# Two maxima of the first layer moved into the projections' bank in tiles 5 and 6, and 26 unread products taken out

## The chip, the cores and the metric

The kernel runs on one core of a Trainium2 chip. The metric is the device time of one execution in microseconds. TensorE is called PE, VectorE DVE, ScalarE ACT, GpSimd POOL and the engine that issues the loads SP, as in the profile.

## What is computed

A perceiver of two layers works on 128 query rows of width 256 against a context of 12544 rows. Each layer begins with a cross attention of 16 heads of width 16; in the first a mask is added to the scores. Between the attentions lie a causal linear attention, a GELU block and a ternary feed-forward block; behind the second lie an RWKV mixing and a ternary convolution block.

```python
q = split_heads(ln(x) @ Wq.T + bq)               # 128 rows
k = split_heads(ctx @ Wk.T + bk)                 # 12544 rows
v = split_heads(ctx @ Wv.T + bv)
scores = einsum('bhqd,bhkd->bhqk', q / 4, k)     # first layer: + (1 - mask) * -10000
out = einsum('bhqk,bhkd->bhqd', softmax(scores), v)
x = x + L0_xattn; x = x + L0_attn; x = x + L0_ffn
x = x + L1_xattn; x = x + L1_attn; x = x + L1_ffn
```

## The kernel before

The context is cut into NB = 14 blocks of 896 rows, each into 7 tiles of 128. Blocks are numbered m = 0 to 27: 0 to 13 in the first layer, 14 to 27 in the second. The softmax runs online: before the scores of a block are computed, its maximum over the 896 rows is needed for every head and query. It comes from 32 **maxima** a block (16 heads, two halves of 448 rows): `maximum` on PE (L1081) multiplies the high halves of queries and keys into a bank of PSUM, and DVE reduces that to one column (L753, with the mask added, in the first layer; L756 in the second). Here `J` counts them, and `max_free` says that DVE has read one.

The maxima of block m+1, and the first of block m+2, are spread over the tiles of block m. A tile is, in PE's order: `scores` (the row maxima subtracted, L1118, then the scores, L1122), the maxima "behind the scores", `weigh` (the values weighed with the probabilities of the tile before, L1139), the maxima "behind the weighing", `projections` (keys L1064 in tiles 0, 2, 4, 6, values L1054 in tiles 1, 3, 5, in the bank `ps_proj`; in tile 5 a piece of the values before that into a lent bank of `ps_scores`, and in tile 6 four products that turn the new maxima, L1156, into the same lent bank), and the maxima "ahead", always two. In tile 1 the sums of the block before are turned in `ps_proj` (L1150), and DVE adds them (L802). `count_at` gives the numbers by tile from `SCORED_AT` and `WEIGHED_AT`. All engines follow one table, `MAXIMA`; `MAX_BANK` says which bank a product goes to: 0 and 1 are the two halves of `ps_max`, used in turn, 2 is `ps_proj`, which then has to be free of its last reader (`proj_free`).

The other engines in a tile of the first layer: DVE adds the mask to the scores of eight heads (L811), ACT copies the other eight (L539) and POOL adds the mask to them (L426); ACT takes the exponentials (L546), copies keys (L507), values (L514) and sums (L530) out of PSUM. At tile 5 DVE makes the chain of the block's maximum: L769, L772, L779. POOL besides prepares the mask (L395), the ternary weights (L407, L409, L411), the high halves of the keys (L417) and decays the sums (L437). A load into a mask or context buffer is issued by SP in the order of the blocks, and waits for the last use of that buffer.

Block 13 has no maxima and no projections; its scores alternate between banks, and DVE adds all of the mask (L822). Between the layers, projections for blocks 15, 16, 14 and 15 fill PE's waits (`between_in`). The first maxima of the second layer are read in pairs of halves (`pair_maximum`, L764).

`idle_products(n, bank)` (L1211) issues n products of 128x256 fp32 that nobody reads; each is two records in the trace.

Of the kernel before, what the change touches and what calls it, by code (L numbers as in the profile page):

```python
# [17 lines left out]
TILES = 7  # L18
KB = TILES * P
NB = SK // KB  # L20
# [15 lines left out]
def perceiver(nc, a, out):  # L36

    with ExitStack() as ctx:
# [13 lines left out]
        ps_proj = ctx.enter_context(nc.psum_tensor("ps_proj", [P, 512], F32))  # L52
# [127 lines left out]

        SCORED_AT = ((2, 0, 2, 1, 2, 0, 0), (2, 1, 2, 2, 2, 2, 2))
        WEIGHED_AT = ((1, 2, 1, 2, 1, 2, 2), (0, 2, 1, 1, 0, 1, 0))
        LAST_AT, SUMS_AT = 5, 1
# [17 lines left out]
        for l in range(2):  # L201
            done, read = {NB * l: 2 * H}, {bank: 2 * H * (NB * l + 1) for bank in range(2)}
            turn_of = 0
            for m in range(NB * l, NB * (l + 1)):
                for t in range(TILES):
                    now, ahead = count_at(m, t)
                    MAXIMA[m, t] = []
                    for k in range(3):
                        here = []
                        for to, count in ((m + 1, now[k]), (m + 2, ahead[k])):  # L210
                            at = done.get(to, 0)
                            here += [(to, j) for j in range(at, at + count)]
                            done[to] = at + count
                        for i, (to, j) in enumerate(here):
                            if m > 0 and k == 0 and len(here) == 2 and i == 0 and (t != SUMS_AT or m == NB):
                                MAX_BANK[to, j] = 2
                            else:
                                MAX_BANK[to, j], MAX_AFTER[to, j] = turn_of, read[turn_of]
                                read[turn_of] = 2 * H * to + j + 1
                                turn_of = 1 - turn_of  # L220
                        MAXIMA[m, t].append(here)
# [469 lines left out]
        def _(dve):  # L691
# [140 lines left out]
            for l in range(2):  # L832
# [26 lines left out]
                for n in range(NB):  # L859
                    m = NB * l + n  # L860
                    for t in range(TILES):
                        behind_scores, behind_weighing, ahead = MAXIMA[m, t]
                        early = behind_scores if l == 1 or m == 0 else behind_scores[0:1]
                        for k, j in early:
                            maximum(k, j)
                        if l == 0 and is_last(m):
                            bias_last(m, t)
                        elif l == 0:
                            bias_first(m, t)
                        for k, j in behind_scores[len(early):]:  # L870
                            maximum(k, j)
# [157 lines left out]
        def _(pe):  # L1029
# [97 lines left out]
            def weigh(m, t):  # L1127
# [7 lines left out]
                for half in (first, 1 - first):  # L1135
                    pe.wait_ge(sig(f"exp_done{half}"), T + 1)
                    for j, h in enumerate(HEADS[half]):
# [3 lines left out]
                                  skip_group_check=True)  # L1141
                    if m == NB - 1 and half == first and SUMS_AT <= t < TILES - 1:
                        proj_free(None)
                        idle_products(1, ps_proj)
                last.then_inc(sig("pv_done"), 1)
# [73 lines left out]
            for l in range(2):  # L1219
# [32 lines left out]
                else:  # L1252
                    for i in range(H):
                        pair_maximum(NB, i)
                        if i in BESIDE_AT:
                            beside_in(BESIDE_AT.index(i))
                        elif i > 5:
                            idle_products(1, ps_out)
                        if i == 5:
                            for u in range(len(BESIDE)):  # L1260
                                beside_read(u)
                read_by[0] = ("max_copied", NB * l + 1)
                idle_products(2 + 2 * l, ps_proj)
                turn_max(NB * l)
# [4 lines left out]
                for n in range(NB):  # L1269
                    m = NB * l + n  # L1270
                    for t in range(TILES):
# [18 lines left out]
                        for k, j in ahead:  # L1290
                            maximum(k, j)
                if l == 0:
                    idle_products(2, ps_proj)
                weigh(NB * l + NB - 1, TILES - 1)
# [6 lines left out]
                if l == 0:  # L1301
# [48 lines left out]
                    between_in(10, 11, 12)  # L1350
                    idle_products(1, ps_proj)
                    pe.wait_ge(sig("hq_made"), 1)
                    for c in range(FC):
                        last = tr(ps_max[:, 0, :].bitcast(BF16)[:, P * c:P * (c + 1)], xq[:, P * c:P * (c + 1)], ident16[:, :])
                    last.then_inc(sig("hq_turned"), 1)
                    idle_products(2, ps_proj)
                    pe.wait_ge(sig("hq_ready"), 1)
# [115 lines left out]
```

## Time and profile before

| what | value |
|---|---|
| three runs | 1075.67, 1073.76, 1072.72 us (median 1073.76) |
| profiled execution | 1068.03 us, its span 1066.3 us |
| mean granted clock of PE | 0.992 |
| busy, share of the span | PE 95%, DVE 70%, ACT 64%, POOL 39% |
| DMA | 53.31 MB, mean 50 GB/s |
| a block of the first layer | 33.73 us |

The profile is of one execution. The granted clock is 1 where PE runs at its full 2.4 GHz and 0.5 where it runs at 1.2. A PE that is called busy is not PE at its peak: the ends of products are modelled, and neighbours overlap.

### The profile page before, as it was taken

How to read it: one execution, taken by the hardware profiler on the slowest of the kernel's cores; microseconds unless marked ns; L12 is line 12 of the kernel's file. 1: busy time of each engine (PE TensorE's matmuls, PEld its weight loads, DVE VectorE, ACT ScalarE, POOL GpSimd, SP SyncE). 2: the span in 40 equal slices, each digit the busy share in tenths (PEclk: the TensorE clock that was granted, in tenths of full speed). 3: DMA queues.
4: the chain of work that ended last, by engine and by line, in shares of the span. 5: the costliest groups of instructions: out<-in, count | busy, mean ns of one | idle time of the engine just before them, and what ended most of it. 6: DMA issues, size and time to landing. Idle time of an engine off the chain costs nothing. (4 is left out here: it accounts for less than half of the span.)

```text
span 1066.3 us, 30777 instructions
## 1 busy us (share of the span) xinstructions
PE 1017.6 (95%) x12921; PEld 687.8 (65%) x12921; DVE 743.1 (70%) x1715; ACT 679.0 (64%) x953; POOL 420.8 (39%) x374
## 2 busy tenths in 40 slices
PE   8899999999999999998878899999999999999876
PEld 5466666676666666665544566667676666666665
DVE  4888888888888888876357666556665565566465
ACT  3677777777778777876542555566556666555722
POOL 4368888888888988881000000101100101000000
PEclk9999999999999999999998999999999999999999
DMA  8420122201221112112031010111100111000000
GB/s 313 140 71 20 54 70 71 67 23 53 71 72 34 45 65 70 53 66 93 10 120 68 2 36 2 37 36 37 36 8 30 37 37 36 2 2 2 2 1 5
DMA packets 14682, 53.31 MB, mean 50 GB/s; under 512 B 3025, under 2 KB 4817, under 8 KB 13649
## 3 DMA queue, kind: packets, MB, share of 16 engines
q1 hardware_dynamic: 14544, 51.35, 14.0%
q8 instruction: 102, 1.67, 0.7%
q14 instruction: 36, 0.29, 0.1%
HBM read 51.21 MB, written 0.13 MB: 48 GB/s over the span
## 5 line engine op out<-in xcount | busy, mean ns | idle before, releaser
L756 DVE TENSOR_REDUCE tile_max<-ps_max 128x1 f32<-128x448 f32 x339 | 200.7, 620 | 150.7 <-PE ps_max L1081 146.5
L753 DVE CUSTOM_DVE_ANT_0 unread<-ps_max,masks 128x448 bf16<-128x448 f32 x396 | 231.4, 621 | 67.4 <-PE ps_max L1081 66.2
L426 POOL TENSOR_TENSOR probs<-probs,masks 128x512 f32<-128x512 f32 x182 | 228.1, 1275 | 72.0 <-ACT probs L539 70.5
L551 ACT ACTIVATE probs<-ps_scores 128x1024 f32<-128x1024 f32 x193 | 187.2, 1021 | 86.2 <-PE ps_scores L1122 86.1
L546 ACT ACTIVATE probs<-probs 128x1024 f32<-128x1024 f32 x196 | 207.4, 1058 | 54.5 <-DVE probs L811 45.7
L1122 PE MATMUL ps_scores<-q_pad,k_full 32*128 32x256 f32 x3088 | 230.6, 377 | 0.0
L1139 PE MATMUL ps_out<-probs,values 128*32 128x128 f32 x6272 | 214.5, 277 | 0.7 <-ACT probs L551 0.4
L1139 PEld LDWEIGHTS ps_out<-probs,values 128*32 128x32 f32 x6272 | 159.4, 110 | 51.7 <-issue 48.0
L1122 PEld LDWEIGHTS ps_scores<-q_pad,k_full 32*128 32x128 f32 x3088 | 191.4, 186 | 0.7
L1081 PE MATMUL ps_max<-k_high,q_high 32*128 32x448 bf16 x735 | 180.1, 358 | 7.9 <-DVE tile_max L756 5.3
L1064 PE MATMUL ps_proj<-ctx_t,wk 128*128 128x448 f32 x384 | 168.8, 562 | 0.0
L417 POOL CAST k_high<-k_full 128x896 bf16<-128x896 f32 x56 | 52.3, 935 | 262.1 <-ACT k_full L507 262.1
L1054 PE MATMUL ps_proj<-wv,ctx_t 128*128 128x256 f32 x608 | 148.9, 388 | 0.0
L1081 PEld LDWEIGHTS ps_max<-k_high,q_high 32*128 32x128 bf16 x735 | 48.4, 91 | 140.8 <-issue 70.2
L1054 PEld LDWEIGHTS ps_proj<-wv,ctx_t 128*128 128x128 f32 x608 | 111.3, 190 | 23.4 <-issue 8.0
L811 DVE TENSOR_TENSOR probs<-ps_scores,masks 128x1024 f32<-128x1024 f32 x91 | 111.1, 1221 | 1.6 <-PE ps_scores L1122 1.4
L1118 PE MATMUL ps_scores<-max_rows,minus 32*128 32x512 bf16 x772 | 103.8, 382 | 4.8 <-ACT max_rows L525 3.4
L514 ACT COPY values<-ps_proj 128x512 f32<-128x512 f32 x76 | 44.5, 586 | 98.5 <-PE ps_proj L1054 98.3
L539 ACT COPY probs<-ps_scores 128x512 f32<-128x512 f32 x182 | 97.3, 589 | 1.5 <-PE ps_scores L1122 1.4
L1064 PEld LDWEIGHTS ps_proj<-ctx_t,wk 128*128 128x128 f32 x384 | 65.1, 189 | 50.1 <-issue 43.7
L432 POOL TENSOR_TENSOR max_step<-max_wide 128x16 f32<-128x16 bf16 x28 | 6.9, 246 | 225.5 <-DVE max_wide L779 225.5
L507 ACT ACTIVATE k_full<-ps_proj,bk 128x448 f32<-128x448 f32 x96 | 60.9, 635 | 40.3 <-PE ps_proj L1064 38.2
(258 smaller groups left out, 914.4 us busy)
## 6 DMA issues: line engine op xcount, KB each, us to landing
ctx_t<-in_ctx_t SPq DMA_DIRECT2D x28, 896.0 KB, 5.3
masks<-in_mask_n SPq DMA_DIRECT2D x14, 448.0 KB, 3.4
masks<-in_mask_t SPq DMA_DIRECT2D x14, 448.0 KB, 3.5
room_w<-in_L_attn_f_w SPq DMA_DIRECT2D x2, 1024.0 KB, 7.5
room_w<-in_L_ffn_w SPq DMA_DIRECT2D x2, 1024.0 KB, 8.8
room_w<-in_L_ffn_w_gate SPq DMA_DIRECT2D x1, 1024.0 KB, 10.6
room_w<-in_L_ffn_w_up SPq DMA_DIRECT2D x1, 1024.0 KB, 13.1
room_w<-in_L_ffn_w_down SPq DMA_DIRECT2D x1, 1024.0 KB, 15.0
```

The costliest lines, as they stand in the source:

```text
L426: nc.gpsimd.tensor_tensor(p, p, three(mask_t[m % 2], TILES)[:, t, :].unsqueeze(1).to_broadcast([P, 4, P]), ALU.add).then_inc(sig("bias_add ...
L546: nc.scalar.activation(prob(T, half), prob(T, half), ACT.Exp).then_inc(sig(f"exp_done{half}"), 1)
L551: nc.scalar.activation(prob(T, half), scores_half(T, half), ACT.Exp).then_inc(sig(f"exp_done{half}"), 1)
L753: ins = v.tensor_tensor_reduce(unread[:, j % 2, :], max_bank(m, j)[:, 0:HALF], mask_n[m % 2][:, HALF * half:HALF * (half + 1)], 1.0, -3e38 ...
L756: ins = v.tensor_reduce(tile_max[:, h, half:half + 1], max_bank(m, j)[:, 0:HALF], AX_X, ALU.max)
L811: v.tensor_tensor(prob(T, 0).rearrange("p (h q) -> p h q", h=8), ps_scores[:, 0:2, :].rearrange("p a (h q) -> p (a h) q", q=P), three(mask ...
L1054: last = mm(bank[:, D * (t - at.start):D * (t - at.start + 1)], ctx_t[m % 3][:, c, P * t:P * (t + 1)], wv[l][:, c, :], start=(c == 0), sto ...
L1064: last = mm(bank[:, 0:HALF], wk[l][:, c, P * oc:P * (oc + 1)], ctx_t[m % 3][:, c, HALF * half:HALF * (half + 1)], start=(c == 0), stop=(c ...
L1081: mm(max_bank(m, j)[:, 0:HALF], q_high[rows, c, zz, :], k_high[m % 2][rows, c, HALF * half:HALF * (half + 1)], start=True, stop=True).then ...
L1118: mm(banks[g], minus16[rows, :], max_rows[m % 2][rows, :], start=True, stop=True)
L1122: last = mm(banks[g][:, D * c:D * (c + 1)], k_full[m % 3][rows, c, P * t:P * (t + 1)], q_pad[rows, c, :], start=False, stop=True, skip_gro ...
L1139: last = mm(ps_out[VW * g:VW * (g + 1), P * c:P * (c + 1)], values[m % 2][:, t, h, :], prob(T, half)[:, P * o:P * (o + 1)], start=(t == 0 ...
```

## The change

Per block of the first layer, the maxima behind the weighing fall from 1 to 0 in tiles 0 and 2, and those behind the scores rise from 0 to 1 in tiles 5 and 6; their total stays 32. The function `late_bank` sends the ones of tiles 5 and 6 into `ps_proj`, and `before_mask` has DVE read them behind its mask addition. The functions `idle_products` in block 13 (5 products), among the pairs (10), before the turning of the first maxima (2 and 4), before the last weighing of the first layer (2) and around the gated products (3) are taken out. Those of the tail remain, as do the small products (`idents`) at the start.

```diff
-        SCORED_AT = ((2, 0, 2, 1, 2, 0, 0), (2, 1, 2, 2, 2, 2, 2))
-        WEIGHED_AT = ((1, 2, 1, 2, 1, 2, 2), (0, 2, 1, 1, 0, 1, 0))
+        SCORED_AT = ((2, 0, 2, 1, 2, 1, 1), (2, 1, 2, 2, 2, 2, 2))
+        WEIGHED_AT = ((0, 2, 0, 2, 1, 2, 2), (0, 2, 1, 1, 0, 1, 0))
+        def late_bank(m, t):
+            return m < NB and t >= LAST_AT
+
+        def before_mask(m, t, count):
+            return 0 if late_bank(m, t) else count if m == 0 or m >= NB else min(count, 1)
...
-                            if m > 0 and k == 0 and len(here) == 2 and i == 0 and (t != SUMS_AT or m == NB):
+                            if k == 0 and (late_bank(m, t) or m > 0 and len(here) == 2 and i == 0 and (t != SUMS_AT or m == NB)):
                                 MAX_BANK[to, j] = 2
...
-                        early = behind_scores if l == 1 or m == 0 else behind_scores[0:1]
-                        for k, j in early:
+                        early = before_mask(m, t, len(behind_scores))
+                        for k, j in behind_scores[:early]:
                             maximum(k, j)
...
-                        for k, j in behind_scores[len(early):]:
+                        for k, j in behind_scores[early:]:
                             maximum(k, j)
...
-                    if m == NB - 1 and half == first and SUMS_AT <= t < TILES - 1:
-                        proj_free(None)
-                        idle_products(1, ps_proj)
...
-                        elif i > 5:
-                            idle_products(1, ps_out)
...
-                idle_products(2 + 2 * l, ps_proj)
...
-                if l == 0:
-                    idle_products(2, ps_proj)
...
-                    idle_products(1, ps_proj)
                     pe.wait_ge(sig("hq_made"), 1)
...
-                    idle_products(2, ps_proj)
                     pe.wait_ge(sig("hq_ready"), 1)
```

## Rows read from the trace of the kernel before

**Rows 1.** Busy time by stretch: block 7 of the first layer, its tile 6; columns: stretch, length, busy.

```profile
310.12:343.86 33.74, 33.51 (x453) 22.57 (x454) 28.36 (x75) 26.43 (x39) 27.93 (x24) 1.00 0.17 57
...
339.01:343.86 4.85, 4.63 (x69) 2.81 (x70) 3.40 (x9) 4.05 (x6) 3.50 (x5) 1.00 0.21 80
```

**Rows 2.** Timeline, tiles 0 to 3 of block 7: start, duration, engine, line, tiles.

```profile
312.51 0.36 PE L1081 MATMUL ps_max<-k_high,q_high 32*128 32x448 bf16 x1
...
312.79 1.77 PE L1064 MATMUL ps_proj<-ctx_t,wk 128*128 128x448 f32 x4
...
314.50 0.46 PE L1081 MATMUL ps_max<-k_high,q_high 32*128 32x448 bf16 x2
...
314.70 0.47 PE L1118 MATMUL ps_scores<-max_rows,minus 32*128 32x512 bf16 x4
...
314.93 0.64 ACT L507 ACTIVATE k_full<-ps_proj,bk 128x448 f32<-128x448 f32 x1
...
315.97 0.66 PE L1150 MATMUL ps_proj<-ident,out_t 128*128 128x128 f32 x4
...
319.79 0.36 PE L1081 MATMUL ps_max<-k_high,q_high 32*128 32x448 bf16 x2
...
319.80 0.57 PE L1118 MATMUL ps_scores<-max_rows,minus 32*128 32x512 bf16 x4
...
324.24 0.38 PE L1081 MATMUL ps_max<-k_high,q_high 32*128 32x448 bf16 x2
...
324.36 0.48 PE L1118 MATMUL ps_scores<-max_rows,minus 32*128 32x512 bf16 x4
```

**Rows 3.** Timeline, tiles 5 and 6 of block 7.

```profile
335.76 2.50 POOL L426 TENSOR_TENSOR probs<-probs,masks 128x512 f32<-128x512 f32 x2
...
336.23 0.62 DVE L753 CUSTOM_DVE_ANT_0 unread<-ps_max,masks 128x448 bf16<-128x448 f32 x1
...
336.77 0.62 DVE L753 CUSTOM_DVE_ANT_0 unread<-ps_max,masks 128x448 bf16<-128x448 f32 x1
...
337.66 0.64 DVE L772 TENSOR_SCALAR block_max<-block_max 128x16 f32<-128x16 f32 x1
338.23 1.50 POOL L411 TENSOR_SCALAR tern<-room_w 128x512 bf16<-128x512 f32 x1
...
341.81 0.62 DVE L753 CUSTOM_DVE_ANT_0 unread<-ps_max,masks 128x448 bf16<-128x448 f32 x1
...
341.95 0.40 PE L1156 MATMUL ps_scores<-ident,max_wide 128*128 128x128 bf16 x4 [0.22 <-DVE probs L811]
...
342.19 1.72 PE L1064 MATMUL ps_proj<-ctx_t,wk 128*128 128x448 f32 x4
```

**Rows 4.** Timeline, a tile of block 13.

```profile
491.56 2.19 ACT L546 ACTIVATE probs<-probs 128x1024 f32<-128x1024 f32 x2 [0.78 <-DVE probs L822]
...
493.27 2.35 DVE L822 TENSOR_TENSOR probs<-ps_scores,masks 128x1024 f32<-128x1024 f32 x2 [0.61 <-PE ps_scores L1122]
...
493.57 0.70 PE L1211 MATMUL ps_proj<-wq,ident 128*128 128x256 f32 x2
...
494.20 0.65 PE L1139 MATMUL ps_out<-probs,values 128*32 128x128 f32 x16
```

**Rows 5.** Timeline, DVE in the pairs before the second layer's first block.

```profile
563.21 2.08 DVE L764 TENSOR_REDUCE tile_max<-ps_scores 128x2 f32<-128x896 f32 x2
...
569.42 2.20 DVE L764 TENSOR_REDUCE tile_max<-ps_scores 128x2 f32<-128x896 f32 x2
```

**Rows 6.** Busy time by stretch, with PE's clock; the last two are of PE alone.

```profile
34.90:38.30 3.40, 2.10 (x19) 1.37 (x22) 1.82 (x9) 3.01 (x6) 1.12 (x2) 1.00 0.54 153
...
574.90:579.03 4.13, 2.11 (x29) 1.14 (x27) 1.56 (x3) 2.63 (x4) 0.91 (x2) 1.00 0.00 0
...
579.86:586.25 6.39, 5.67 (x59) 0.50 0.01 3
...
591.76:595.86 4.10, 3.51 (x60) 1.00 0.02 4
```

## The prediction

> **What bounds it now.** I read first the busy times by stage, then each engine's timeline through one block of the first layer, then the stretches around the removed products. In a block PE is busy 33.51 of 33.74 us, DVE 28.36, ACT 26.43, POOL 27.93 [rows 1]. So PE's order of work sets the pace of blocks 1 to 12, and a product taken out of PE's stream is worth its slot, as long as DVE, ACT and POOL, four fifths full, don't hold the next product. Only tile 6 has a hole in PE: there it is busy 4.63 of 4.85 us [rows 1]. Around the layers PE waits for others; there the removed products lie, and they cost slots in two places only.
>
> **Part 1: tiles 0 and 2 lose their middle maximum.** In tile 0 the lone product behind the weighing starts at 312.51, the keys' projection at 312.79: a slot of 0.29 us (the two starts unrounded) [rows 2]; tile 2 has the same pair. A second effect: of the pair behind the projection the second product waits for the bank that the middle maximum held. In tile 0 the scores start 0.20 us behind that pair, in tile 2 0.12, where after tile 1 it is 0.01 [rows 2]. Without the middle maximum both banks are free, so tile 0 may gain up to 0.29 + 0.19 = 0.48, tile 2 0.29 + 0.11 = 0.40. What is late next in tile 0 is ACT: its keys copy runs 314.93 to 315.57, behind other work of ACT, and releases the turning of the sums, now at 315.97 [rows 2]; the bank allows at most 315.62, so 0.35 of the 0.48 arrives. Tile 2 has no such turn: I take 0.39. Together -0.74 a block; bounds 0 (ACT and DVE pass nothing on) and -0.88.
>
> **Part 2: one maximum more in tiles 5 and 6, in ps_proj.** Behind the scores PE takes one in at nearly no slot: it sits on 32 rows that the scores leave one after another. Bounds 0 and the 0.29 of a slot; I take 0.05, nearer to the scores' own packing, and in tile 6 it is hidden by PE's hole. But DVE reads it only behind the mask addition, and the next projection writes the same bank.
> In tile 5 the values' projection into the lent score bank comes first, so ps_proj is free in time. DVE's two later reads and the chain move back: the mask addition ends the DVE stretch and the reads stand 0.54 to 0.55 apart (336.23, 336.77) [rows 3]; with the new one in front, which DVE can start some 0.17 before the present first, the second old read moves by 0.38 to 337.15, and L772, now 337.66, is issued at about 338.04. There it matters that L772 runs 0.64 us: it ends at 338.30, just behind POOL's pair of additions (335.76 + 2.50 = 338.26) [rows 3]. It is blocked until then already, so arriving at 338.04 it ends at the same 338.30 and the 0.38 costs nothing. The margin is 0.22.
> In tile 6 nothing hides it. DVE's next read behind the mask addition starts at 341.81, PE's turning products, which wait for that addition, at 341.95, the keys at 342.19 [rows 3]. The new read takes the place at 341.81, ends about 0.55 + 0.08 later, and only at 342.50 can the keys write ps_proj: +0.31 us, on the path, since PE has nothing else queued. Everything behind it (the pair ahead, its reads, the scores of the next tile 0) moves with it. The bounds are 0 and the whole read plus a handover, 0.65.
> The sum by blocks: blocks 1 to 11, 11 x (-0.74 + 0.31 + 0.01) = -4.6; block 12, which has no maximum ahead in tile 6, -0.7; block 0, only tile 6, +0.3. Together -5.0 us. The 0.05 of tile 5 mostly falls into the wait of the borrowed bank, hence 0.01. No DMA and no wait of SP is moved: the mask's next load waits for the same count of maxima, an SP step with a block of slack.
>
> **A rule that speaks against it.** L772 is seen held up to POOL's end in the trace [rows 3]. The Trainium skill, SBUF — State Buffer, section "Who interferes with whom", says that the engine that issues first gets the port pair that DVE and POOL share for its whole instruction. The trace agrees for L772. By that rule a link that came after 338.26 would sit behind POOL's next instruction; this is rival B.
>
> **Part 3: 26 unread products.** Each is two records; one takes a slot of 0.63 us in block 13 (493.57 to 494.20) [rows 4]. There ACT's two exponentials end at 493.75 and the second half of the weighing starts at 494.20 [rows 4]; without the product it can start at 493.80. That half and the scores two tiles on come 0.40 earlier, 0.20 a tile, for five tiles: -1.0. DVE isn't reached: its two additions take 2.35 us and it is idle 0.61 before them [rows 4]. Before layer 2's first block two of DVE's double reads take 2.08 us at the start of the row of pairs and 2.20 late in it [rows 5], so spacing 1.00 against 1.11: PE paces the last six: -0.6. Four more products end at about 574.84 and hold the turning by 0.15. Together -1.7; bounds 0 and -2.2. The others lie in waits: 2 behind the first maxima, 2 before the last weighing (ACT is late there), 3 around the gated products. Each is free, and cover is lost for one thing only, the clock.
>
> **Part 4: the clock.** After 574.90 to 579.03, in which PE was busy 2.11 of 4.13 us, the granted clock fell to its lower level, 1.2 of 2.4 GHz. The tile from 579.86 then took 6.39 us at 0.50, where a full-clock one took 4.10 [rows 6]: 0.36 us lost for each us of low clock inside tiles. The stretch 34.90 to 38.30 shows 2.10 of 3.40 busy at clock 1.00 [rows 6]; without its two products some 1.1 remain, emptier than the stretch before which the clock fell. Likewise before the last weighing (two products fewer, PE then waits for ACT twice), around the gated products (three fewer), and through the sixteen pairs (ten plus four fewer). I expect more low stretches in each, but not always. Price of one: at 34.90 3 to 10 us low, 1.2 to 3.7 lost, over half of the runs, some of which have it already: +1.0. At 502, the turning and four projections in front of the normed vector: +1.2 (0 to 2). At 546: +0.4 (0 to 1.5). At the pairs DVE paces, so only the first tile's scores and the turning are late, and the low stretch that follows now may only come sooner: +0.4 (-1 to 1.8). Sum +3.0, bounds 0 and 9.
> TensorE: Matmul & The Clock Gate in the Trainium skill, section "What's actually happening", says that activity releases the throttle, the low level being the default. By this alone all four places would fall every time, and the sum would be at its upper end.
>
> **The sum.** -5.0 - 1.7 + 3.0 = -3.7 us. The profiled execution took 1068.03 (span 1066.3 and 1.7 around it); it gives 1064.3. The median of the three runs is 1073.76, 5.7 us above the profiled one, probably with a low stretch more; the terms apply to them as well: 1073.76 - 3.7 = 1070.0.
>
> **Rivals.**
> A. The clock eats the gain (0.25). For it: four emptied places [rows 6]. Against: the long blocks are dense and untouched. With 6 to 9 us lost, 1073 to 1076, no change or slightly slower.
> B. The chain misses its place behind POOL (0.08; this is the one that ends slower). Place: L772 in tile 5 of blocks 1 to 12. If DVE arrives more than 0.22 us later than I count, POOL's next instruction, 1.50 us from 338.23 [rows 3], runs first; L772 then ends at 339.9 instead of 338.30, 1.6 later. DVE's wait for the pair ahead takes up some of that; I take four fifths, 1.3, for the mask addition of tile 6, the turning and the keys. 12 x 1.3 = +15.6: about 1086. It decides from 0.22 us on; below, nothing.
> C. ACT and DVE pass on nothing of tiles 0 and 2 (0.10): the 0.31 x 12 = +3.7 stands alone, 3.7 - 1.7 + 3.0 = +5.0, 1078.8. Against: PE's 99% in the block [rows 1].
> D. The clock costs nothing (0.17): -6.7, 1067.1.
> The forecast itself, the gain in the blocks and a middling clock, has 0.40, with a range of its own of 1068 to 1072.
>
> **Range and chances.** About 0.3% (3.2 us) is what a measurement of this kernel can tell from no change. From D's 1067 with a little more from the bounds of part 1 (1065.5), up to A and C (1079); B is left out with the tails. Faster: D and four fifths of the forecast, 0.50. Same: the rest of it and most of A, 0.30. Slower: B, C and a little of A, 0.20.
>
> **What would show it.** Tile 0 and tile 2 about 0.35 to 0.4 shorter, tile 6 0.3 longer, tile 5 equal; the block 33.3 instead of 33.74. L772 still ending with POOL's additions. Block 13 near 2.8 us a tile. DVE's pairs spaced 1.00. Low stretches at one or more of 36, 503, 546 and from 565 on. It would be wrong if tile 0's gain stopped at ACT's copy, if the keys of tile 6 waited longer than 0.3, or if low stretches lay inside the blocks.

## The result and the profile after

The changed kernel takes 1068.43 us (median of 20 runs, 1064.00 to 1072.92), the kernel before 1072.39 (20 runs, 1067.88 to 1075.67). The ratio is 0.996, with an interval of 0.9944 to 0.9976: 4.0 us or 0.4% faster. The forecast was 1070.0 from 1073.76, a gain of 3.7.

The two profiled executions say nothing of the kind: 1067.97 us after, 1068.03 before, the span 1066.3 in both. Their granted clocks differ, 0.978 against 0.992. Before's profile is one of its quickest runs, after's is an ordinary one. So I compare the two by stretches first, and take the clock up separately.

A tile's length is taken from the first score product (L1118 before, L1125 after: all lines of this kernel stand 7 lower in the changed one) to that of the next tile. Counted from block 0, the block of [rows 1] is block 8; the text ahead calls it 7. Blocks 1 to 11 are alike (but for tile 6 of block 4, 0.35 longer in both), so nothing hangs on it.

| us | t0 | t1 | t2 | t3 | t4 | t5 | t6 | block |
|---|---|---|---|---|---|---|---|---|
| before | 4.58 | 5.09 | 4.57 | 4.60 | 4.59 | 5.46 | 4.85 | 33.73 |
| after | 4.10 | 5.21 | 4.16 | 4.62 | 4.53 | 5.48 | 5.19 | 33.29 |

Busy time by stretch of the changed kernel; the block and tile 1 of it, then the stretch ahead of block 0 and its first tile, the turning of block 13's sums with the keys behind it, the stretch from the gated products to the second layer's query products, the pairs. Columns: stretch, length, busy PE, PEld, DVE, ACT, POOL, granted clock, DMA share, GB/s.

```profile
309.84:343.13 33.29, 32.94 (x452) 22.30 (x451) 27.83 (x75) 26.25 (x39) 27.90 (x24) 1.00 0.17 58
313.93:319.14 5.21, 5.21 (x70) 3.80 (x70) 3.84 (x10) 4.21 (x7) 4.60 (x5) 1.00 0.08 30
...
34.90:38.30 3.40, 1.24 (x12) 0.70 (x14) 1.90 (x9) 3.09 (x6) 1.12 (x2) 1.00 0.50 149
38.09:45.50 7.41, 6.50 (x32) 2.52 (x34) 3.40 (x9) 2.13 (x3) 2.50 (x2) 0.54 1.03 337
501.50:504.50 3.00, 3.00 (x7) 1.74 (x6) 2.12 (x6) 0.87 (x2) 0.00 (x0) 0.50 0.00 0
549.00:556.00 7.00, 4.44 (x14) 2.13 (x13) 2.23 (x9) 1.92 (x5) 0.00 (x0) 0.74 0.90 320
560.00:576.00 16.00, 11.63 (x38) 3.14 (x36) 14.47 (x16) 2.50 (x3) 0.00 (x0) 0.71 0.20 68
```

The block is 0.44 shorter, PE still fills it [rows 1], and the clock is 1.00 in it. All that went against the gain lies around the layer: PE is busy for 1.24 us of the stretch at 34.90 instead of 2.10 [rows 6], and behind it the first tile of block 0 runs at 0.54 and takes 7.41 us where it took 5.22. By starts: block 13 begins 2.83 earlier than before (475.62 against 478.45), which is +0.09 at the start, +2.71 in block 0, 11 x -0.44 in blocks 1 to 11 and -0.79 in block 12. Block 14 begins 1.77 later (577.67 against 575.90): -0.6 in the tiles of block 13 and +5.2 behind them. Block 14 is equal (31.91 against 31.89). In the rest before has two short low stretches and after one, -1.8. The sum is -0.06, the difference of the two profiled times.

Timeline of the changed kernel, tiles 0 and 1 of the block, which answers to [rows 2].

```profile
311.21 1.08 PE L1146 MATMUL ps_out<-probs,values 128*32 128x128 f32 x32
...
312.22 1.77 PE L1071 MATMUL ps_proj<-ctx_t,wk 128*128 128x448 f32 x4
...
313.93 0.36 PE L1088 MATMUL ps_max<-k_high,q_high 32*128 32x448 bf16 x2
...
313.93 0.57 PE L1125 MATMUL ps_scores<-max_rows,minus 32*128 32x512 bf16 x4
...
314.63 0.64 ACT L514 ACTIVATE k_full<-ps_proj,bk 128x448 f32<-128x448 f32 x1
...
315.32 0.42 PEld L1154 LDWEIGHTS ps_proj<-ident,out_t 128*128 128x128 f32 x4 [0.35 <-ACT k_full L514]
315.32 0.66 PE L1154 MATMUL ps_proj<-ident,out_t 128*128 128x128 f32 x4
```

The keys follow the weighing with no lone product between; the pair ahead and the next scores now start together (they stood 0.20 apart in [rows 2]), the whole 0.48. Then the turning stands behind ACT's copy of the keys, which ends at 315.27, and tile 1 is 0.12 longer: 0.36 of 0.48 arrives.

The same kernel, tiles 5 and 6, which answers to [rows 3].

```profile
334.71 2.51 POOL L433 TENSOR_TENSOR probs<-probs,masks 128x512 f32<-128x512 f32 x2
...
334.99 0.61 DVE L760 CUSTOM_DVE_ANT_0 unread<-ps_proj,masks 128x448 bf16<-128x448 f32 x1
...
336.73 0.19 DVE L776 TENSOR_REDUCE block_max<-tile_max 128x16 f32<-128x32 f32 x1
336.95 0.30 DVE L779 TENSOR_SCALAR block_max<-block_max 128x16 f32<-128x16 f32 x1
337.19 1.50 POOL L418 TENSOR_SCALAR tern<-room_w 128x512 bf16<-128x512 f32 x1
337.29 0.59 DVE L786 TENSOR_TENSOR max_wide<-block_max,max_wide 128x16 bf16<-128x16 f32 x1
...
339.60 1.22 DVE L818 TENSOR_TENSOR probs<-ps_scores,masks 128x1024 f32<-128x1024 f32 x1
...
340.74 0.61 DVE L760 CUSTOM_DVE_ANT_0 unread<-ps_proj,masks 128x448 bf16<-128x448 f32 x1
...
340.88 0.40 PE L1160 MATMUL ps_scores<-ident,max_wide 128*128 128x128 bf16 x4 [0.21 <-DVE probs L818]
341.28 0.08 DVE L760 DVE_READ_ACCUMULATOR2_ANT tile_max<- 128x1 f32 x1
...
341.42 0.30 PEld L1071 LDWEIGHTS ps_proj<-ctx_t,wk 128*128 128x128 f32 x2 [0.32 <-DVE tile_max L760]
341.42 1.77 PE L1071 MATMUL ps_proj<-ctx_t,wk 128*128 128x448 f32 x4
```

In tile 5 the link of the chain that [rows 3] shows 0.64 long is issued late and takes 0.30: it still ends (337.25) with POOL's additions (337.22). In tile 6 the keys wait for DVE's read of `ps_proj`, which the trace names as their releaser; they start 0.54 behind the turning, before 0.24 [rows 3].

The clock is the other half. All four places that the forecast named fell: in the profile after the low stretches begin at 38.66 (6.83 us long), 499.45 (6.83), 547.24 and 554.07 (3.41 and 6.83) and 567.72 (20.48). Before had one of these, 10.24 us from 579.03.

### The profile page after: what moved, and what is told of

It is laid out like the page before. It is cut to its first block and busy times, and to the rows that moved or that the text cites. A ratio compares the mean times of both kernels' runs of the same rounds, so it can differ in the third digit from the quotient of the medians.

```text
span 1066.3 us, 30674 instructions
## 1 busy us (share of the span) xinstructions
PE 1007.3 (94%) x12869; PEld 678.9 (64%) x12869; DVE 736.4 (69%) x1715; ACT 676.7 (63%) x953; POOL 420.4 (39%) x374
## 5 line engine op out<-in xcount | busy, mean ns | idle before, releaser
L760 DVE CUSTOM_DVE_ANT_0 unread<-ps_max,masks 128x448 bf16<-128x448 f32 x372 | 218.2, 621 | 71.5 <-PE ps_max L1088 71.4
L1129 PE MATMUL ps_scores<-q_pad,k_full 32*128 32x256 f32 x3088 | 233.1, 377 | 0.0
L1129 PEld LDWEIGHTS ps_scores<-q_pad,k_full 32*128 32x128 f32 x3088 | 194.0, 186 | 0.8
L1088 PE MATMUL ps_max<-k_high,q_high 32*128 32x448 bf16 x711 | 169.6, 359 | 8.1 <-DVE tile_max L763 5.3
L1071 PE MATMUL ps_proj<-ctx_t,wk 128*128 128x448 f32 x384 | 171.0, 568 | 1.7
L1088 PEld LDWEIGHTS ps_max<-k_high,q_high 32*128 32x128 bf16 x711 | 44.3, 91 | 137.4 <-issue 63.3
L1125 PE MATMUL ps_scores<-max_rows,minus 32*128 32x512 bf16 x772 | 106.2, 382 | 4.9 <-ACT max_rows L532 3.4
```

Source lines behind the costliest of these rows:

```text
L760: ins = v.tensor_tensor_reduce(unread[:, j % 2, :], max_bank(m, j)[:, 0:HALF], mask_n[m % 2][:, HALF * half:HALF * (half + 1)], 1.0, -3e38 ...
L1071: last = mm(bank[:, 0:HALF], wk[l][:, c, P * oc:P * (oc + 1)], ctx_t[m % 3][:, c, HALF * half:HALF * (half + 1)], start=(c == 0), stop=(c ...
L1088: mm(max_bank(m, j)[:, 0:HALF], q_high[rows, c, zz, :], k_high[m % 2][rows, c, HALF * half:HALF * (half + 1)], start=True, stop=True).then ...
L1125: mm(banks[g], minus16[rows, :], max_rows[m % 2][rows, :], start=True, stop=True)
L1129: last = mm(banks[g][:, D * c:D * (c + 1)], k_full[m % 3][rows, c, P * t:P * (t + 1)], q_pad[rows, c, :], start=False, stop=True, skip_gro ...
```

## The experiments

The edit is shown against the changed kernel, and for the last two of the second group against the version before them. Where several runs were made, the ratio is to the kernel before on the same chip, whose medians in the four comparisons were 1072.03, 1073.15, 1069.52 and 1075.14. "Low time" is what the granted clock says of a run, twice (1 - clock) of its span; its mean is 26 us for before (18 runs) and 46 for the changed kernel (20 runs). What one profile says of the clock is said of one execution.

### The two parts by themselves

Schedule alone, all 26 products back:

```diff
+                    if m == NB - 1 and half == first and SUMS_AT <= t < TILES - 1:
+                        proj_free(None)
+                        idle_products(1, ps_proj)
...
+                        elif i > 5:
+                            idle_products(1, ps_out)
...
+                idle_products(2 + 2 * l, ps_proj)
                 turn_max(NB * l)
...
+                if l == 0:
+                    idle_products(2, ps_proj)
...
+                    idle_products(1, ps_proj)
...
+                    idle_products(2, ps_proj)
```

> The changed order of the maxima with all 26 unread products back. My theory: a block of the first layer takes 33.29 us as in the changed kernel (33.73 before), block 13 keeps its 2.97 us a tile, nothing changes in the clock's chances, so the time is 5.3 us under the kernel before (11 x 0.44 + 0.8 in block 12 - 0.3 in block 0): ratio 0.9950. The rival, that the products' removal is what brought the 4.0 us measured: ratio 0.998 or more here.

Measured: 1064.28 us (1060.61 to 1065.28), ratio 0.992 (0.9892 to 0.9948). Blocks 1 to 11 are 33.29, a tile of block 13 2.97, mean low time 22 us. The gain is 7.8 us and not the 5.3 expected; part of the 2.5 beyond it is the clock, as worked out below. Its profile is low for 6.83 us from 40.04, in block 0, with all products in place.

Products alone, the old schedule (`SCORED_AT`, `WEIGHED_AT` and the reading order of before):

```diff
-        SCORED_AT = ((2, 0, 2, 1, 2, 1, 1), (2, 1, 2, 2, 2, 2, 2))
-        WEIGHED_AT = ((0, 2, 0, 2, 1, 2, 2), (0, 2, 1, 1, 0, 1, 0))
+        SCORED_AT = ((2, 0, 2, 1, 2, 0, 0), (2, 1, 2, 2, 2, 2, 2))
+        WEIGHED_AT = ((1, 2, 1, 2, 1, 2, 2), (0, 2, 1, 1, 0, 1, 0))
```

> The old order of the maxima with the 26 unread products out. My theory: block 13 gains 0.6 us (2.82 a tile), the pairs 0.5, and more low stretches of the clock cost about 2 to 3, so +0.5 to +2.5 us: ratio 1.000 to 1.0025. Rival one, the clock costs nothing: -1.7 us, ratio 0.998. Rival two, the clock eats 6 us or more: ratio above 1.004.

Measured: 1071.65 us (1068.98 to 1075.09), ratio 1.0004 (0.9982 to 1.0025); a tile of block 13 2.82, mean low time 42 us. Two of its twelve runs, 3300.33 and 1412.36 us, far from all others of any kernel here, are left out; with them the median is 1072.1. Taking the products out gives nothing that could be measured; what it saves in slots is lost again, and the low time says that the clock takes it. The gain is the schedule's.

### Which products were holding the clock

The 7 products that lie in waits put back (2 at the first maxima, 2 before the last weighing, 3 around the gated products):

```diff
+                if l == 0:
+                    idle_products(2, ps_proj)
                 turn_max(NB * l)
...
+                if l == 0:
+                    idle_products(2, ps_proj)
...
+                    idle_products(1, ps_proj)
...
+                    idle_products(2, ps_proj)
```

> The changed kernel with 7 products put back into PE's waits (2 behind the first maxima, 2 before the last weighing, 3 around the gated products); those of block 13 and of the pairs stay out. My theory: they cost no slot and take back most of the low stretches near 36, 502 and 546, 2 us on average, so about 6 us under the kernel before: ratio 0.9944. The rival, that low stretches come there with or without them: as the changed kernel, 0.996.

Measured: 1063.0 us (1061.19 to 1068.84), ratio 0.9923 (0.9891 to 0.9955), mean low time 35 us. In its profile the low stretches of 502 and 546 are gone, but that of block 0 is not: 6.83 us from 40.54, and the block takes 38.57 us. There the two products don't hold the clock every time.

The 14 among and behind the pairs put back:

```diff
+                        elif i > 5:
+                            idle_products(1, ps_out)
...
+                if l == 1:
+                    idle_products(4, ps_proj)
```

> The changed kernel with the 14 unread products of the pairs back (10 between them, 4 before the turning), the other 12 out. My theory: in 20 runs of the changed kernel the clock was low for 46 us, in 18 of the one before for 26; most of the difference lies in the pairs, where DVE paces and low clock is cheap. With the products the pairs' low stretch goes or shortens (low time near 32 us), DVE's spacing is 1.11 again (+0.6), and the first tiles of block 14 gain back 1 to 2 us: 0 to 1.5 us under the changed kernel, ratio 0.995. The rival, that the pairs' products cost more than the clock there: 0.997 or more.

Measured: 1065.13 us (1063.95 to 1072.01), ratio 0.9943 (0.9921 to 0.9966), low time 32 us. The first two tiles of block 14, 5.40 and 6.39 in the changed kernel, came down with it, to 3.96 and 5.59 (the block 29.67 against 31.91).

Both, that is all but block 13's five:

```diff
+                        elif i > 5:
+                            idle_products(1, ps_out)
...
+                idle_products(2 + 2 * l, ps_proj)
...
+                if l == 0:
+                    idle_products(2, ps_proj)
...
+                    idle_products(1, ps_proj)
...
+                    idle_products(2, ps_proj)
```

> The changed order of the maxima, all unread products of the kernel before except the 5 of block 13. My theory: schedule -5.3 to -6.2, block 13 -0.6, low clock as before: 6.0 to 6.8 us under the kernel before at equal low time, ratio 0.994, low time 22 to 26 us. The rival, that block 13's products protect the clock: its tiles or the last weighing show low clock and the ratio is no better than that of the schedule alone.

Measured: 1061.28 us (1059.67 to 1067.59), ratio 0.9914 (0.9881 to 0.9946), low time 20 us, a larger gain than the 0.994 expected. The rival is out: neither the tiles of block 13 nor the last weighing show low clock. Block 0 took 35.98 us; it is 38.35 in the changed kernel and 35.64 before.

To that, 11 more products in waits that had none: around block 0's and block 14's first scores and between the second layer's query products.

```diff
+                else:
+                    idle_products(1, ps_scores[:, 3, :])
...
+                else:
+                    idle_products(2, ps_scores[:, 3, :])
...
+                if l == 1:
+                    idle_products(1, ps_scores[:, 3, :])
...
+                    idle_products(2, ps_scores[:, 3, :])
+                else:
+                    idle_products(1, ps_out)
...
+                        if n == 0 and t == 0:
+                            idle_products(2, ps_out if l else ps_proj)
```

> The kernel of the run before with all unread products but block 13's, and 11 more unread products in waits of PE: 4 around the first scores of block 0, 4 between the second layer's query products, 3 around the first scores of block 14. My theory: the low stretches near 40, 551 and 575 go or get rarer, low time falls from 20 to 10 us on average, at some 0.4 us per us that is 4 us less, less up to 1 us for products that reach out of their waits: 3 us under that kernel, 1058, ratio 0.988 to 0.989. The rival, that products in such short waits delay more than the clock gives: 0.9914 or more.

Measured: 1059.3 us (1056.7 to 1066.78), ratio 0.9909 (0.9872 to 0.9947), low time 12 us. Busy time by stretch in its profile, the places that were low in the changed kernel (the last row is the pairs from the third read on):

```profile
38.00:45.00 7.00, 6.80 (x53) 3.86 (x57) 4.58 (x15) 3.99 (x8) 3.05 (x3) 1.00 0.93 346
500.00:507.00 7.00, 6.22 (x23) 4.10 (x22) 5.18 (x15) 2.83 (x7) 0.93 (x1) 1.00 0.00 0
555.40:569.40 14.00, 13.76 (x54) 6.07 (x53) 13.87 (x16) 1.87 (x2) 0.00 (x0) 1.00 0.30 107
```

PE is busy 13.76 of 14.00 us in the pairs, 11.63 of 16.00 in the changed kernel, and the clock stays at 1.00. Block 14 takes 28.36 us in place of 31.91, with no tile above 4.14. Its interval doesn't part it from the version above it.

Three products more, at the start of block 13, since four of the eight runs were slower (1060.78 and 1065.33 to 1066.78):

```diff
+                        if m == NB - 1 and t < 2:
+                            proj_free(None)
+                            idle_products(1 + t, ps_proj)
```

> The kernel of the run before with 3 more unread products in the waits of block 13 (one behind its first scores, two behind the second). Its slower runs had a clock of 0.990, and one look at another kernel showed low clock from 485, with 1.6 us more in block 13. My theory: that place is emptied by the end of the projections, and with products there the low time falls below 10 us and no run is above 1062: ratio 0.988. The rival, that the products lengthen block 13 (3.11 and 4.31 us for its first tiles) or that the slower runs have another place: as the run before, 0.991.

Measured: 1062.7 us (1057.54 to 1066.21), ratio 0.9891 (0.9856 to 0.9926). Three of six runs still stand at a clock of 0.990 and 1064.59 to 1066.21, so I was wrong on the place: the profile, itself one of the slower kind, is low for 17.07 us from 558.89, through the pairs. Its mean low time is 14 us, not under 10. The two rows are the granted clock in 40 slices of the span, first of the version with 11 more, then of this one; the digit 6 is the slice that begins at 558.

```profile
PEclk9999999999999999999999999999999999999999
```

```profile
PEclk9999999999999999999996999999999999999999
```

This fall came although the waits were filled: PE was busy 3.15 of the 3.39 us before it, and 3.50 of 3.50 before those.

```profile
555.50:558.89 3.39, 3.15 (x13) 1.12 (x12) 3.39 (x4) 1.71 (x2) 0.00 (x0) 1.00 0.94 326
```

```profile
562.75 1.09 DVE L771 TENSOR_REDUCE tile_max<-ps_scores 128x2 f32<-128x896 f32 x1 [0.92 <-PE ps_scores L1099]
```

And here the unread products make it dear. With one of them behind each pair, DVE's reads stand 1.11 apart at full clock but 2.01 at the lower one, and DVE waits 0.92 for PE each time; without them it was 1.00 at either level. From the start of block 13 to that of block 14 this profile takes 104.63 us, that of the version with 11 more 96.91: 7.7 us for 17.07 us low. What lets the clock fall in about half the runs of either version stays open, and whether it falls in the pairs in the others too: only the profiled ones show the place.

One profile was kept of each of the fourteen kernels. Counted over them, how many fell at each place, with its products in and without:

| products | low stretch | in | out |
|---|---|---|---|
| 2 behind the first maxima | near 40 | 2 of 6 | 8 of 8 |
| 2 before the last weighing | 23 to 27 us behind the start of block 13 | 0 of 6 | 7 of 8 |
| 3 around the gated products | 69 to 82 us behind the start of block 13 | 2 of 6 | 8 of 8 |
| 14 among and behind the pairs | one of more than 20 us | 0 of 6 | 8 of 8 |

So at each of the four places the products make a fall (in the pairs a long one) rarer. They don't rule it out: at two places it came with them, and in the pairs one of 17.07 us did.

### Where the two maxima can stand

Only one moved, tile 2's into tile 5 (one execution):

```diff
-        SCORED_AT = ((2, 0, 2, 1, 2, 1, 1), (2, 1, 2, 2, 2, 2, 2))
-        WEIGHED_AT = ((0, 2, 0, 2, 1, 2, 2), (0, 2, 1, 1, 0, 1, 0))
+        SCORED_AT = ((2, 0, 2, 1, 2, 1, 0), (2, 1, 2, 2, 2, 2, 2))
+        WEIGHED_AT = ((1, 2, 0, 2, 1, 2, 2), (0, 2, 1, 1, 0, 1, 0))
```

> Only tile 2's middle maximum moved (to tile 5); tile 0 keeps its own and tile 6 gets none; no unread products as in the changed kernel. My theory: tiles 0, 1 and 6 are as before the change (4.58, 5.09, 4.85), tile 2 4.16; the block takes 33.3 us as with both moved, since what tile 0 gives (0.48 less 0.12 in tile 1) tile 6 takes (0.34). The rival, that both moves pay: 33.5 or more.

Measured, tiles: 4.58 5.09 4.16 4.62 4.53 5.48 4.85, block 33.31; the changed kernel has 33.29. (Its time, 1070.6 us, is with 51 us of low time.) Tile 5 takes its maximum for 0.02 and that buys 0.41 in tile 2 (and tile 4 is 0.06 shorter with it). The other move gives 0.48 - 0.12 in tile 0 and 1 and costs 0.34 in tile 6: 0.02 of net gain. One of the two moves carries the whole gain.

Tile 6's maximum in tile 3 in its place, behind the scores:

```diff
-        SCORED_AT = ((2, 0, 2, 1, 2, 1, 1), (2, 1, 2, 2, 2, 2, 2))
+        SCORED_AT = ((2, 0, 2, 2, 2, 1, 0), (2, 1, 2, 2, 2, 2, 2))
```

> The changed kernel with the maximum of tile 6 put behind the scores of tile 3 instead (two there, none in tile 6). My theory, that in tile 6 the keys wait for the bank that DVE reads late: tile 6 falls from 5.19 back to 4.85 us, tile 3 grows by 0.1 at most, a block takes 33.0 us, 3 us less over twelve blocks: ratio 0.9932. The rival, that DVE is then the bound of tile 3 (six reads and the mask addition are 4.4 us of 4.6): tile 3 or 4 grows by 0.3 or more and the time is that of the changed kernel, 0.996.

Measured: 1082.38 us (1077.61 to 1083.87), ratio 1.0085 (1.0053 to 1.0117). Tile 6 is back at 4.85, as expected, but tile 3 takes 6.16, 1.54 more, beyond even the rival's 0.3 or more. Its timeline in the same block:

```profile
333.05 0.35 PE L1088 MATMUL ps_max<-k_high,q_high 32*128 32x448 bf16 x1
...
334.07 1.22 DVE L818 TENSOR_TENSOR probs<-ps_scores,masks 128x1024 f32<-128x1024 f32 x1
...
334.39 0.36 PE L1088 MATMUL ps_max<-k_high,q_high 32*128 32x448 bf16 x1
...
335.21 0.61 DVE L760 CUSTOM_DVE_ANT_0 unread<-ps_max,masks 128x448 bf16<-128x448 f32 x1
335.75 0.08 DVE L760 DVE_READ_ACCUMULATOR2_ANT tile_max<- 128x1 f32 x1
...
335.89 0.36 PE L1088 MATMUL ps_max<-k_high,q_high 32*128 32x448 bf16 x1 [1.15 <-DVE tile_max L760]
336.18 1.59 PEld L1061 LDWEIGHTS ps_proj<-wv,ctx_t 128*128 128x128 f32 x8 [0.20 <-issue]
```

The second maximum behind the scores (333.05) goes to `ps_max`, and DVE reads it only at 335.21, behind the mask addition. The second of the two behind the weighing needs that bank, and PE stands still for 1.15 us in front of it, with the values' projection queued behind. The rival named the right engine, for DVE works without a gap from 332.34 to this read, but what PE waits for is this one bank. A maximum is cheap for PE where it stands in line; what it costs is how long its bank is held, and by whom.

Tile 6's new maximum read by DVE ahead of the mask addition (one execution):

```diff
-            return 0 if late_bank(m, t) else count if m == 0 or m >= NB else min(count, 1)
+            return 0 if late_bank(m, t) and t == LAST_AT else count if m == 0 or m >= NB else min(count, 1)
```

> The changed kernel, but DVE reads the maximum of tile 6 ahead of its mask addition, not behind it. My theory: tile 6 hangs on DVE's mask addition, which releases the turning products; with the read in front it comes 0.55 later, the keys no longer wait for the bank but for the turning, and tile 6 takes 5.35 to 5.4 us (5.19 with the read behind, 4.85 without the maximum). The rival, that DVE has room ahead of the mask addition: 4.9 to 5.0 us.

Measured: tile 6 5.39, block 33.48 (the time, 1074.02 us, with 56 us of low time). Timeline in the same block, where tile 6 begins at 340.59:

```profile
342.26 0.62 DVE L760 CUSTOM_DVE_ANT_0 unread<-ps_proj,masks 128x448 bf16<-128x448 f32 x1
...
342.80 1.22 DVE L818 TENSOR_TENSOR probs<-ps_scores,masks 128x1024 f32<-128x1024 f32 x1
```

```profile
344.08 0.40 PE L1160 MATMUL ps_scores<-ident,max_wide 128*128 128x128 bf16 x4 [0.75 <-DVE probs L818]
344.31 1.72 PE L1071 MATMUL ps_proj<-ctx_t,wk 128*128 128x448 f32 x4
```

The keys stand right behind the turning again, 0.23, so the bank's wait is gone; but the addition and with it the turning come 0.55 later, 3.49 into the tile in place of 2.94. Read late, the maximum delays the keys alone by 0.30; read early, it delays the turning by the whole read. That the tile pays 0.34 for it is the cheaper of the two.

### The chain and POOL

One unread reduction of 128x256 on DVE ahead of the chain (one execution):

```diff
+                if 0 < m < NB:
+                    v.tensor_reduce(stat[:, 40:41], wq[0][:, 0, 0:256], AX_X, ALU.max)
```

> The changed kernel with one more reduction on DVE (128x256, read by nobody, some 0.45 us) ahead of the chain in tile 5 of the first layer's blocks. Rival B of the prediction and my margin of 0.22 to 0.27 us say: L779 (L772 before) is issued 0.19 behind the end of POOL's additions and waits for the whole of POOL's ternary instruction: it ends 1.6 us later, tile 6 grows by 0.8 to 1.3 us, about 12 us in all. If instead a late link only waits its turn, the chain ends 0.2 later and tile 6 stays at 5.19.

Measured: 1067.99 us, tile 6 5.19, block 33.29, all as in the changed kernel. Its timeline, one block earlier in the same trace:

```profile
303.44 0.42 DVE L777 TENSOR_REDUCE stat<-wq 128x1 f32<-128x256 f32 x1
303.78 0.18 DVE L778 TENSOR_REDUCE block_max<-tile_max 128x16 f32<-128x32 f32 x1
303.90 1.50 POOL L418 TENSOR_SCALAR tern<-room_w 128x512 bf16<-128x512 f32 x1
303.99 0.55 DVE L781 TENSOR_SCALAR block_max<-block_max 128x16 f32<-128x16 f32 x1
304.58 0.23 DVE L788 TENSOR_TENSOR max_wide<-block_max,max_wide 128x16 bf16<-128x16 f32 x1
```

The link now comes 0.09 behind the start of POOL's next instruction, the case of rival B. It should end at 305.40 with it; it ends at 304.54, 0.64 behind its start, and the next link runs freely within it. Two such reductions, so that the link comes later still (one execution):

```diff
+                if 0 < m < NB:
+                    v.tensor_reduce(stat[:, 40:41], wq[0][:, 0, 0:256], AX_X, ALU.max)
+                    v.tensor_reduce(stat[:, 42:43], wq[0][:, 0, 0:256], AX_X, ALU.max)
```

> The changed kernel with two such reductions ahead of the chain, some 0.9 us. The run with one showed L781 issued behind the start of POOL's ternary instruction and ending 0.64 us after that start, not at its end, and the next link at full speed. If DVE is held only for the first 0.64 us or so of such an instruction, L783 is issued near its end and takes 0.2 us, the chain ends some 0.4 later than with one reduction, 0.3 of it reaches the reads, and tile 6 takes 5.2 to 5.5 us. If a link that comes in the middle is held to the instruction's end, it ends 0.9 later and tile 6 takes 6 us or more.

```profile
303.97 1.50 POOL L418 TENSOR_SCALAR tern<-room_w 128x512 bf16<-128x512 f32 x1
304.17 0.18 DVE L779 TENSOR_REDUCE block_max<-tile_max 128x16 f32<-128x32 f32 x1
304.38 0.23 DVE L782 TENSOR_SCALAR block_max<-block_max 128x16 f32<-128x16 f32 x1
304.64 0.23 DVE L789 TENSOR_TENSOR max_wide<-block_max,max_wide 128x16 bf16<-128x16 f32 x1
```

These rows are of the same block as those above. Issued 0.41 behind POOL's start the link takes 0.23, though POOL goes on until 305.47. Where nothing of POOL runs beside it, this link takes 0.17 to 0.18; so it is still held a little, and ends 0.64 behind POOL's start, where it ended in the run before. In the one block where it comes 0.46 behind that start it is not held at all:

```profile
204.17 0.17 DVE L782 TENSOR_SCALAR block_max<-block_max 128x16 f32<-128x16 f32 x1
```

The chain thus ends no later than with one reduction (28.26 us into the block in both), and tile 6 stays at 5.19, a little under the 5.2 to 5.5 expected. The time is 1067.9 us. Both kernels do reductions on DVE that nobody reads; nothing else is changed.

## Why the prediction was right

**The blocks: right, to 0.02 a block.** Forecast -0.42 (-0.74 + 0.31 + 0.01), measured -0.44. Tile 0 and 1 together -0.36 (forecast -0.35), stopped by ACT's copy of the keys as part 1 says (its own list of signs calls just that a sign of being wrong, which contradicts its sum); tile 2 -0.41 (-0.39); tile 5 +0.02; tile 6 +0.34 (+0.31), with the releaser foreseen. Tile 4, of which I said nothing, is 0.06 shorter. Block 12 gained 0.79 (0.7) and block 0's tile 6 lost 0.34 (0.3). The sum over the blocks, without what the clock did to block 0, is -4.8 - 0.8 + 0.3 = -5.3, forecast -5.0. The early read and the maximum in tile 3 show that tile 6's price comes from who holds the bank; the move of one maximum shows that this price eats the gain of tile 0 and 1 but for 0.02.

**Rival B: its lateness came true as counted, its mechanism isn't there.** The link is issued at 336.95; POOL's additions end at 337.22, a margin of 0.27 (forecast 0.22). With the margin used up, nothing came of it. The trace of before could have told this: the third link there, L779, meets L411 in the same way. The rows above show it for the changed kernel, L786 issued 0.10 behind the start of L418, 0.59 long, and ended 0.81 before the end of L418. By the rule of the Trainium skill, SBUF — State Buffer, "Who interferes with whom", it should have been held to POOL's end. The trace agrees behind POOL's mask addition: the link L772 (L779 after) ends 0.03 behind it in each of the twelve blocks of both profiles. It doesn't agree behind POOL's `tensor_scalar` of 128x512, where the links that were held ended 0.63 to 0.78 us after its start, while it ran for 1.49 to 2.01. What ends the hold there is open; the profile's spans on POOL are rough.

**Part 3: right in sign, the term for block 13 too large.** "For five tiles: -1.0" assumed 0.20 a tile. Measured is 2.97 to 2.82, 0.15, in four tiles: -0.6. The pairs are spaced 1.00 from the third read to their end, as said (-0.55): DVE's double reads take 2.08 at 562.50 and 2.08 still at 571.48 (the first one and the last).

```profile
562.50 2.08 DVE L771 TENSOR_REDUCE tile_max<-ps_scores 128x2 f32<-128x896 f32 x2
...
571.48 2.08 DVE L771 TENSOR_REDUCE tile_max<-ps_scores 128x2 f32<-128x896 f32 x2
```

The 0.15 for the turning behind them no run shows by itself: from the last read to block 14 it is 3.15 us before and 3.20 after, at the lower clock.

**Part 4: right on the places, too sure that a fall is optional, and the price per place unequal.** I left each place a chance to hold; in the profile all four fell, and none of the 20 runs has less than 38 us of low time (before: from 15). Without their products the four places fell in 31 of 32 cases of the table above. So the rule that I cited from the Trainium skill, TensorE: Matmul & The Clock Gate, "What's actually happening", by which all four fall every time, is the better account of how often. Its upper end of 9 us did not come, because low time isn't of one price. Over the runs of before (18) and of the schedule alone (6), one slope fits both: 0.43 us per us of low time (standard error 0.02, residual 0.6 us, the largest 1.8), a fifth above the 0.36 worked out from one tile. But the places differ. Block 0 paid 2.7 us for its 6.83 us low, 0.40 each; between block 13's tiles and block 14 the profile after is low for 27 us where before isn't, and pays 5.2 net, 0.19 each. In the pairs DVE sets the pace from the third read on: the spacing is 1.00 there, in the low stretch from 567.72 too (the last row above). But the forecast's "only the first tile's scores and the turning are late" missed one gap, between the second read and the third, where a projection of keys stands between PE's products. In the low stretch from 554.07 it takes 3.36 us (1.77 before), DVE waits 2.41 for PE (0.43 before), and the gap is 3.49 us instead of 1.51. First the row of before, then two of after:

```profile
559.21 1.09 DVE L764 TENSOR_REDUCE tile_max<-ps_max 128x2 f32<-128x896 f32 x1 [0.43 <-PE ps_max L1092]
```

```profile
557.52 3.36 PE L1071 MATMUL ps_out<-ctx_t,wk 128*128 128x448 f32 x4
...
561.49 1.09 DVE L771 TENSOR_REDUCE tile_max<-ps_max 128x2 f32<-128x896 f32 x1 [2.41 <-PE ps_scores L1099]
```

So the row of pairs as a whole, from its first read to its last, grew from 16.06 to 17.48 us.

The net of parts 3 and 4 was forecast as +1.3. Measured, it is within 0.4 of zero with the old schedule (products alone against before, by median or ratio) and +4.2 with the new one (1068.43 against 1064.28, from two separate comparisons); either is uncertain by some 3 us each way, and the forecast is within both. The schedule is worth -7.8 us by its own comparison. Of the 2.5 us beyond -5.3 the clock, low for 22 us and not 26, makes 4 x 0.43 = 1.7; at equal low time the mean times of the two kernels differ by 6.2 (standard error 0.3). What makes the rest, some 0.9 us beyond the tiles, is open, and so is why the products cost 4.2 us with one schedule and nothing with the other, if the difference is real. So the forecast's total is right with its terms apart: by these runs the schedule gained 2.8 more than its -5.0, and parts 3 and 4 cost 2.9 more than their +1.3. In the blocks the mechanisms held; but that the total came within 0.3 us, with two errors of nearly 3 us that cancel, is luck.

**Rivals.** C (nothing passed on) and B are out by the tiles. D (the clock costs nothing) is out: the first tile of block 0 lost 2.2 us to it, and the changed kernel is slower than its schedule alone. A was half true: with the slots saved (1.2 by the tiles and pairs) added to the 0 and 4.2, the clock takes 1.2 to 5.4 us, and not the whole gain. Had the change kept its 21 unread products outside block 13, it would probably have been better than it is: 1061.28, and with eleven more 1059.3. Those intervals touch the changed kernel's, 0.9881 to 0.9946 and 0.9872 to 0.9947 against 0.9944 to 0.9976; that of the version with three more in block 13, 0.9856 to 0.9926, does not.

**The median and the profile.** I put the 5.7 us between before's profile and its median down to one low stretch more. The runs bear out that it is the clock: at 0.992 before takes 1067.77 to 1068.47 us, at 0.984 1074.68 to 1076.13, 17 us of low time for some 7.5 us. Whether that is one stretch or several, and where, no profile shows.

## What to carry to other kernels

Where PE's order sets the pace, price a small product by its slot and by who holds its bank until when: the same maximum cost 0.02 us in one tile, 0.34 in the next and 1.54 in a third. Unread products in waits make a fall of the clock rarer, though they don't rule it out; before they are taken out, ask what runs right behind each wait, and if it is PE's dense work, leave them. In a row that another engine paces they cost little at full clock (0.11 us a pair), but 1.01 once the clock has fallen. When a change touches the clock, compare tiles and the time against the granted clock of each run, not two profiles: here the two profiled times were equal to 0.1 us, and the medians 4 us apart.

## What the runs showed of the hardware

For the kernel before and the schedule alone a run's time follows its granted clock with a residual of 0.6 us, at 0.43 us for each us at the lower level, and that is most of the 9 us over which the runs of before spread (1066.81 to 1076.13). In the changed kernel's own 20 runs the slope is 0.39 (standard error 0.05) and the residual 1.15. The clock also fell once behind a PE that was busy 3.50 of 3.50 and then 3.15 of 3.39 us. A small DVE instruction of 128x16 (0.17 to 0.23 us alone) that meets a `tensor_scalar` of 128x512 fp32 on POOL is held only up to 0.63 to 0.78 us after that one's start, though POOL runs for 1.49 to 2.01, and not at all where it came 0.46 after it; behind POOL's `tensor_tensor` of 128x512 a `tensor_scalar` of 128x16 is held to the end, and a `tensor_reduce` isn't held (0.19 us). A lone maximum on 32 rows takes a slot of 0.29 us between two products on 128 rows, and lengthened tile 5 by 0.02 behind the scores, which are on 32 rows themselves.
